# A first self-attention whose layer norm moves into its own tile loop: GpSimd normalises three steps ahead, TensorE transposes beside the projections

## The reference, cut to what matters

```python
x = x + _L0_xattn_ref(_layernorm(x), ctx, ctx, mask, ...)      # phase a
x = x + _L0_attn_ref(_layernorm(x), Wq, bq, Wk, bk)            # phase b, the one changed
x = x + _L0_ffn_ref(_layernorm(x), ...)                        # phase f
...                                                            # phases c, d, g

def _layernorm(x, axis=-1, eps=1e-05):
    m = jnp.mean(x, axis=axis, keepdims=True)
    v = jnp.var(x, axis=axis, keepdims=True)
    return (x - m) / jnp.sqrt(v + eps)

def _L0_attn_ref(x, Wq, bq, Wk, bk):
    q = (x @ Wq + bq)...; k = (x @ Wk + bk)...; v = k
    attn = softmax(einsum('bhnd,bhmd->bhnm', q, k) * C ** (-0.5))
    return einsum('bhnm,bhmd->bhnd', attn, v)...
```

## Time and profile before

| | us |
|---|---|
| time, median of 3 runs (2725.26 to 2728.6) | 2725.66 |
| time of the profiled execution | 2725.43 |
| its span, first to last instruction | 2723.5 |
| mean granted TensorE clock, share of full speed | 0.914 |
| TensorE busy / VectorE / ScalarE / GpSimd | 2278.5 / 1625.7 / 1527.4 / 458.0 |

### The profile page before, as it was taken

The page is one execution under the profiler, slowest core; times in us unless marked ns, Lnnn a source line. Parts: engine busy times, 40 slices in busy tenths (PEclk is TensorE's granted clock), DMA queues, the critical chain, the costliest instruction groups (busy, mean ns, idle before and its releaser), DMA issues. The chain is left out here.

```text
span 2723.5 us, 66405 instructions
## 1 busy us (share of the span) xinstructions
PE 2278.5 (84%) x19431; PEld 1622.9 (60%) x19431; DVE 1625.7 (60%) x5236; ACT 1527.4 (56%) x3786; POOL 458.0 (17%) x1104
## 2 busy tenths in 40 slices
PE   5999999979759997999999999997256217499997
PEld 3777777757536765778778778775115103344443
DVE  5888878867554434665665665665798878701100
ACT  5888888867512224555555555554478737532221
POOL 2545445423213320000000000000000030000000
PEclk9999999989869997999999999998698655699999
DMA  3222222200100002111111111111000000100001
GB/s 90 75 74 71 75 71 72 73 27 1 26 0 0 0 1 90 39 46 43 38 46 43 38 46 43 39 46 34 0 0 1 0 1 4 44 1 0 0 0 31
DMA packets 153177, 90.39 MB, mean 33 GB/s; under 512 B 34033, under 2 KB 151169, under 8 KB 152705
## 3 DMA queue, kind: packets, MB, share of 16 engines
q1 hardware_dynamic: 153088, 89.26, 11.3%
HBM read 68.24 MB, written 20.97 MB: 33 GB/s over the span
## 5 line engine op out<-in xcount | busy, mean ns | idle before, releaser
L667 ACT ACTIVATE a_PR<-a_SM,a_nmx 128x257 f32<-128x257 f32 x512 | 253.4, 499 | 4.0 <-issue 3.3
L1039 ACT ACTIVATE c_PR<-c_SM,c_nmx 128x257 f32<-128x257 f32 x512 | 253.3, 501 | 0.0
L963 PE MATMUL c_bs<-c_cT,c_QP 128*128 128x257 f32 x1024 | 247.9, 386 | 0.8 <-ACT c_QP L1027 0.8
L982 PE MATMUL c_bo<-c_PT,c_C 128*128 128x512 f32 x512 | 240.8, 593 | 2.0 <-DVE c_PT L1099 2.0
L1073 DVE CUSTOM_DVE_ANT_0 c_SM<-c_bs,c_MB 128x257 f32<-128x257 f32 x512 | 215.4, 424 | 17.0 <-PE c_bs L963 14.2
L714 DVE CUSTOM_DVE_ANT_0 a_SM<-a_bs,a_MB 128x257 f32<-128x257 f32 x512 | 188.0, 423 | 44.4 <-PE a_bs L535 39.0
L963 PEld LDWEIGHTS c_bs<-c_cT,c_QP 128*128 128x128 f32 x1024 | 186.0, 192 | 25.8 <-issue 1.7
L947 PEld LDWEIGHTS c_bq<-c_XNT,c_A 128*128 128x128 f32 x1024 | 137.6, 196 | 67.2 <-issue 64.0
L1045 ACT ACTIVATE c_OT<-c_bo 128x512 f32<-128x512 f32 x128 | 76.5, 597 | 173.2 <-PE c_bo L982 173.2
L1099 DVE COPY c_PT<-c_bp 128x512 f32<-128x512 f32 x128 | 88.6, 692 | 121.2 <-PE c_bp L971 121.2
L934 POOL TENSOR_TENSOR c_XL<-quarter,c_PR 128x16 f32<-128x16 f32 x128 | 27.6, 216 | 774.3 <-DVE c_PR L1083 774.3
(11 more groups left out here) (492 smaller groups left out, 5252.4 us busy)
## 6 DMA issues: line engine op xcount, KB each, us to landing
a_C<-in_ctx_dram SPq DMA_DIRECT2D x128, 128.0 KB, 2.1
ctxT_dram<-a_cT SPq DMA_DIRECT2D x128, 128.0 KB, 1.9
c_cT<-ctxT_dram SPq DMA_DIRECT2D x128, 128.0 KB, 2.2
c_C<-in_ctx_dram SPq DMA_DIRECT2D x128, 128.0 KB, 2.1
a_MK<-in_mask_Bx1xSxS_bk_dram SPq DMA_DIRECT2D x128, 32.1 KB, 1.9
X<-in_x_dram SPq DMA_DIRECT2D x4, 512.0 KB, 6.4
g_h<-in_L_ffn_h_w_dram SPq DMA_DIRECT2D x2, 1024.0 KB, 7.9
out_dram<-X SPq DMA_DIRECT2D x1, 2048.0 KB, 8.7
```

The costliest lines, as they stand in the source:

```text
L667: nc.scalar.activation(PR[:, 1 - par, hg, :], SM[:, 1 - par, hg, :], ACT.Exp, bias=nmx[:, 1 - par, hg:hg + 1], accum_out=den[:, 1 - par, h ...
L963: nc.tensor.matmul(b_s[hg][:, 0:SK], QP[:, r // 4 % 2, r % 4, 4 * hg:4 * hg + 4, :], cT[:, r, :], start=True, stop=True).then_inc(s_ps, 1)
L982: last = nc.tensor.matmul(b_o[:, :], C[:, buf, c, :], PT[:, s.r % 2, c, :, :], start=(c == 0), stop=(c == 1))
L1039: nc.scalar.activation(PR[:, 1 - par, hg, :], SM[:, 1 - par, hg, :], ACT.Exp, bias=nmx[:, 1 - par, hg:hg + 1], scale=SCALE, accum_out=den[ ...
```

## The change

`phase_norm` is no longer called in phase b. A new function `normaliser` keeps the chain of small operations (without its last, `shift`), and it now runs at the start of the attention block, on VectorE and ScalarE. GpSimd then normalises one tile a step, three steps ahead of its scores: a subtraction into `XS` and a multiplication of `XS` in place, with a wait on its own semaphore between them. TensorE transposes `XS` into a free quarter of the b_bqk bank, ahead of the projections, and ScalarE copies it into `sh.XNT` after `Q`. Steps begin at -3; the loop now covers steps 4 to 27 instead of 4 to 29.

```diff
-        phase_norm(nc, sh, "b_n_", loads, [b_o, b_t])
-            for g in range(-2, 4):
+            for g in range(-3, 4):
                 step(Step(g, g % 2, NT))
-            with eng.Fori(2, NT // 2 - 1) as j:
+            with eng.Fori(2, NT // 2 - 2) as j:
...
-            for g in range(NT - 2, NT + 1):
+            for g in range(NT - 4, NT + 1):
@@ tensor
+                if s.on(-3):
+                    wait(pe, xs_ok, g + 4)
+                    wait(pe, q_ev, g + 2)
+                    wait(pe, k_ev, g + 2)
+                    wait(pe, xt_ev, g + 3)
+                    nc.tensor.transpose(b_qk[:, 2 * P:3 * P], XS[:, 1 - par, :], sh.ident[:, :]).then_inc(xt_ps, 1)
                 if s.on(-2):
                     wait(pe, q_ev, g + 2)
                     wait(pe, k_ev, g + 2)
+                    wait(pe, xt_ev, g + 3)
@@ scalar
+            stats_on_scalar(act)
+                if s.on(-3):
+                    wait(act, xt_ps, g + 4)
+                    nc.scalar.activation(sh.XNT[:, ds(P * (g + 3), P)], b_qk[:, 2 * P:3 * P], ACT.Copy).then_inc(xt_ev, 1)
@@ gpsimd
+            pool.wait_ge(norm_ok, 1)
             def step(s):
                 g, par = s.g, s.r
+                if s.on(-3):
+                    t = g + 3
+                    wait(pool, xt_ps, g + 2)
+                    nc.gpsimd.tensor_tensor(XS[:, 1 - par, :].unsqueeze(1), sh.X[:, ds(t, 1), :],
+                                            mean[:, ds(t, 1)].unsqueeze(2).broadcast_to([P, 1, D]), ALU.subtract
+                                            ).then_inc(xc_ok, 1)
+                    wait(pool, xc_ok, g + 4)
+                    nc.gpsimd.tensor_tensor(XS[:, 1 - par, :].unsqueeze(1), XS[:, 1 - par, :].unsqueeze(1),
+                                            rstd[:, ds(t, 1)].unsqueeze(2).broadcast_to([P, 1, D]), ALU.mult
+                                            ).then_inc(xs_ok, 1)
                 if s.on(-2):
                     wait(pool, k_ev, g + 3)
@@ vector
+            stats_on_vector(dve)
+            dve.sem_inc(norm_ok, 1)
```

More of the change, by code:

```diff
@@ L289, in tile_stats, with normaliser, on_vector, link @@
     nc.vector.bn_stats(sh.stats[:, ds(t, 1), :], sh.X[:, ds(t, 1), :])
+def normaliser(nc, sh, small, chain, var_ok, std):
+    total, mean, diff, dsq, m2, var, rstd, half = (small[:, i, :] for i in range(8))
+    def on_vector(dve):
+        n = 0
+        def link(ins):
+            nonlocal n
+            n += 1
+            ins.then_inc(chain, 1)
+            dve.wait_ge(chain, n)
+        stats = sh.stats
+        link(nc.vector.tensor_tensor(total, stats[:, :, 1], stats[:, :, 4], ALU.add))
+        link(nc.vector.tensor_scalar(mean, total, 0.5, None, ALU.mult))
+        link(nc.vector.tensor_tensor(diff, stats[:, :, 1], stats[:, :, 4], ALU.subtract))
+        link(nc.vector.scalar_tensor_tensor(out=dsq, in0=diff, scalar=0.25, in1=diff, op0=ALU.mult, op1=ALU.mult))
+        link(nc.vector.tensor_tensor(m2, stats[:, :, 2], stats[:, :, 5], ALU.add))
+        link(nc.vector.scalar_tensor_tensor(out=var, in0=m2, scalar=1.0 / D, in1=dsq, op0=ALU.mult, op1=ALU.add))
+        nc.vector.tensor_scalar(var, var, LN_EPS, None, ALU.add).then_inc(var_ok, 1)
+        dve.wait_ge(std, 1)
+        link(nc.vector.reciprocal(rstd, rstd))
+        link(nc.vector.tensor_tensor(half, rstd, rstd, ALU.mult))
+        link(nc.vector.scalar_tensor_tensor(out=half, in0=half, scalar=-0.5, in1=var, op0=ALU.mult, op1=ALU.mult))
+        link(nc.vector.tensor_scalar(half, half, 1.5, None, ALU.add))
+        link(nc.vector.tensor_tensor(rstd, rstd, half, ALU.mult))
+    def on_scalar(act):
+        act.wait_ge(var_ok, 1)
+        nc.scalar.activation(rstd, var, ACT.Sqrt).then_inc(std, 1)
+    def normed(out, t):
+        return nc.vector.tensor_scalar(out, sh.X[:, ds(t, 1), :], mean[:, ds(t, 1)], rstd[:, ds(t, 1)],
+                                       ALU.subtract, ALU.mult)
+    return on_vector, on_scalar, normed
 def phase_xattn0(nc, sh, ctx_rows, mask, wq, bq, wk, bk, wv, bv, wo, bo):
@@ L1114, in phase_attn0 @@
         sh.XNT = sb("b_XNT", [D, T])
+        small = sb("b_small", [P, 8, NT])
+        XS = sb("b_XS", [P, 2, D])
         Q = sb("b_Q", [D, 2, P])
@@ L1134, in phase_attn0, with run, _ @@
         o_ps, r_ok, n_ok, x_ok = sem("b_o_ps"), sem("b_r_ok"), sem("b_n_ok"), sem("b_x_ok")
-        def loads(sp):
+        chain, var_ok, std, norm_ok = sem("b_chain"), sem("b_var_ok"), sem("b_std"), sem("b_norm_ok")
+        xc_ok, xs_ok, xt_ps, xt_ev = sem("b_xc_ok"), sem("b_xs_ok"), sem("b_xt_ps"), sem("b_xt_ev")
+        stats_on_vector, stats_on_scalar, _ = normaliser(nc, sh, small, chain, var_ok, std)
+        mean, rstd = small[:, 1, :], small[:, 6, :]
+        block = ctx.enter_context(nc.Block())
+        def run(eng, step):
+            for g in range(-3, 4):
+                step(Step(g, g % 2, NT))
+            with eng.Fori(2, NT // 2 - 2) as j:
+                for r in range(2):
+                    step(Step(2 * j + r, r, NT))
+            for g in range(NT - 4, NT + 1):
+                step(Step(g, g % 2, NT))
+        @block.sync
+        def _(sp):
             sp.dma_start(wq_s[:, :], wq).then_inc(w_in, 16)
@@ L1140, in loads @@
                 sp.dma_start(bias[:, i:i + 1], v.rearrange("(d a) -> d a", a=1)).then_inc(w_in, 16)
-        phase_norm(nc, sh, "b_n_", loads, [b_o, b_t])
-        block = ctx.enter_context(nc.Block())
-        def run(eng, step):
-            for g in range(-2, 4):
-                step(Step(g, g % 2, NT))
-            with eng.Fori(2, NT // 2 - 1) as j:
-                for r in range(2):
-                    step(Step(2 * j + r, r, NT))
-            for g in range(NT - 2, NT + 1):
-                step(Step(g, g % 2, NT))
         @block.tensor
```

## The result

The changed kernel took 2735.72 us (median of 10 runs, 2731.72 to 2740.31), the kernel before 2725.62 us on the same chip (10 runs, 2719.53 to 2730.78). The ratio is 1.0039, with an interval of 1.003 to 1.0048: slower by 0.39%. The prediction said 2735 us, slower by 0.35%. The profiled execution took 2737.15 us, 1.85 above its span.

The account below looks back on a forecast made before the run. The middle was taken as a TensorE stage; the change would close a round of 3.65 us a step against 3.08. KS of tile 31 comes 9.7 us later: 2725.4 + 9.7 = 2735 us, range 2727 to 2741.

Parts of the forecast that it names:

- The ring: Attention block: round from projections through KS, KP, GpSimd's pair and transpose to projections sets the step, 3.65 us; chance 0.70.
- projections to KS: Term of the ring: from projections issued on TensorE to KS started on ScalarE, 0.84 us.
- KS to KP: Term of the ring: from KS started on ScalarE to KP started on GpSimd, 0.58 us.
- own semaphore and address instruction: Term of the ring: GpSimd's wait on itself, 0.07, and the address instruction behind it, 0.058; 0.13 us.
- hand-over: Term of the ring: from the end of GpSimd's multiplication to TensorE's transpose, 0.14 us.
- transpose to projections: Term of the ring: TensorE's transpose, 0.11, and an assumed 0.06 before the projections can issue; 0.17 us.
- The middle: KS of tile 4 to KS of tile 31: 26 steps of 3.65 plus 3.1, 98.0 us.
- the start: Block start to KS of tile 4, which comes at 615.3 against 620.30: 5.0 of 10.9 us removed are kept.
- ScalarE's round: Rival: ScalarE's work with the new copy sets the step at 3.3 us; time 2726, no change; chance 0.10.
- All hidden: Rival: all added work falls into idle time, the step stays 3.08 us; time 2720.4; chance 0.10.
- The clock: Rival: TensorE, 81% busy, at low clock for half the middle, 5.6 us more; time 2741; chance 0.07.
- Contention at the addition to X: Rival: GpSimd and VectorE hinder each other at VectorE's addition to X, at most 7.5 us more, 2743; chance 0.03.

Follow-up runs that it names:

- x1: Changed kernel with GpSimd's pair (subtraction, multiplication) four steps ahead instead of three; 2719.89 us, ratio 0.9978 to the kernel before.
- x2: Changed kernel with the subtraction of the mean left out, one GpSimd operation instead of two; 2722.93 us, ratio 0.9988 to the kernel before.
- x8: x1 with ScalarE's copy of the transposed tile moved behind the exponential, TensorE's transpose staying ahead of the projections; 2713.72 us, ratio 0.995 to the kernel before.
- x4: Changed kernel with TensorE's transpose of XS at the end of its step and ScalarE's copy behind the exponential; 2715.48 us, ratio 0.9968 to before.
- x7: x4 with x1's edit, GpSimd's pair four steps ahead; 2717.38 us, ratio 0.9964 to the kernel before.
- x6: x4 with one VectorE tensor_scalar behind DS normalising the tile in place of GpSimd's pair; 2726.8 us, ratio 1.0 to the kernel before.
- x9: x6 with VectorE's normalisation at the end of its step, behind the statistics, four steps ahead; 2718.4 us, ratio 0.9968 to the kernel before.
- x3: Changed kernel with a third GpSimd operation, a multiplication by one with its own wait; 2749.94 us, ratio 1.009 to the kernel before.

## Why the prediction was right

**The ring.** It was forecast at 3.70, taken as 3.65, and measured at 3.89 and 3.65 from KS to KS in the two steps shown, 3.71 in the mean of all 27. By its terms:

| term | predicted | measured, the two steps |
|---|---|---|
| projections to KS | 0.84 | 0.83, 0.83 |
| KS to KP | 0.58 | 0.49, 0.59 |
| KP | 1.04 | 1.00, 1.00 (next begins 0.04 ahead of its end) |
| subtraction, multiplication | 0.40, 0.40 | 0.40, 0.41; 0.40, 0.40 |
| own semaphore and address instruction | 0.13 | 0.18, 0.18 |
| hand-over | 0.14 | 0.33, 0.06 |
| transpose to projections | 0.17 | 0.25, 0.19 |
| sum | 3.70 | 3.89, 3.65 |

The first measured column is the round from KS at 649.21 to KS at 653.10, the second the one from KS at 653.10 to KS at 656.75. The first begins with this row, which the two steps above leave out:

```profile
649.21 0.37 ACT L1274 ACTIVATE b_KS<-b_bqk,b_bias 128x128 f32<-128x128 f32 x1 [0.51 <-PE b_bqk L1237]
```

From key to key the loop's steps take 3.65 and 3.87 in turns, 3.76 in the mean, 0.06 above the sum of 3.70; the written-out steps are shorter (3.33 the first), which makes 3.71 over all 27.

**The middle and the start.** The middle was to be 98.0 and was 100.09: 26 steps of 3.73 instead of 3.65, and a last one of 3.04. The terms that were too small are the waits: own semaphore (+0.05), hand-over (+0.06 in the mean) and transpose to projections (+0.05), less 0.09 for KS to KP, KP and the projections. The start was to keep 5.0 us and kept 5.93: KS of tile 0 came 6.85 after the block's start (7.0 predicted), and the four cold rounds took 15.61 (16.4). These two errors nearly cancel, +2.1 and -0.9. The 1.33 us of phase a, which no step of the forecast covers, brings the profiled execution to 2737.15. That the median, 2735.72, came out 0.7 us from the forecast is therefore partly luck: the errors of the parts cancel, and the ten executions spread over 8.6 us. What is borne out is the round and its length, within 0.06 to 0.08 us a step.

**What it named as signs.** TensorE waits at the transpose of XS in 26 steps, 0.40 each ("0.3 or more in nearly every step"), though the trace names GpSimd in 14 of them only. The pair follows KP without a gap. GpSimd's wait for the keys fell to 42.6/24 = 1.78 from 2.05 (1.7 predicted). KS of tile 4 started at 615.70 (615). ScalarE waits ahead of KS 13.7 us in 26 steps, where the list of before has no such wait. One sign fits only in the mean: KS was to come every 3.6 to 3.7 us, and comes every 3.65 and 3.87 in turns.

**The rivals.** ScalarE's round would have set 3.3, at most 3.36; x1 and x2 stop at 3.29, and x8 shows that ScalarE's copy is in what stops them; but it lay 0.42 under the ring. The prediction's reason for this rival, that ScalarE has almost no idle time in the order of the step, is not so; ScalarE waited 0.83 us a step for TensorE before (waits from 620 to 705 us):

```profile
ACT b_ET L1215 <- PE b_bt L1176: 23.3, 28, 1.1
```

It is into this wait that x4, x7 and x8 put the copy. "All hidden" would have needed 0.36 us for the pair, which took 0.98. The clock did not fall in the middle: TensorE was busy 89.21 of 100.09 us, 89% instead of the 81% reckoned, and the granted clock was 1.00 throughout. The transpose that I had costed at 0.11 us of TensorE's step is recorded with 0.326, as it stands alone behind a wait (groups of the middle, changed kernel):

```profile
L1230 PE MATMUL b_bqk<-ident,b_XS 128*128 128x128 f32 x26 | 8.5, 326 | 4.3 <-issue 2.6 <-POOL b_XS L1311 0.3
```

That is 8.5 of the 12.0 us that TensorE's busy time grew in the middle (77.25 in the earlier trace rows). Contention at the addition to X did not show either: at 651.14 above it takes 0.29 with GpSimd's multiplication from 651.28 beside it, and GpSimd's subtraction kept its length (its multiplication took 0.51 once, at the end of the start, and 0.40 in the median):

```profile
L1307 POOL TENSOR_TENSOR b_XS<-X,b_small x32: 397/401/403, 596.8 to 710.9; 128x128 f32 x24, 128x128 f32<-128x128 f32 x8
```

**What stays open.** Why phase a, with unchanged code, is 1.33 us longer here. x1's start is 2.8 us shorter than the changed kernel's; 2.7 of it lie in the two rounds from KS of tile 0 to KS of tile 2, which take 2.45 and 2.29 us instead of 3.74 each.

## What to carry to other kernels

An engine's idle time pays for new work only if it lies ahead of the point at which the result is needed: write the round down, through every in-order engine that the new work ties together, and compare its sum with the step. Look whether work that runs ahead can run one step further. Here it could without any more buffer, since XS has two halves in both kernels and x1 only fills the other one; that turned +0.39% into -0.22%, and with the copy moved into a wait that stood there anyway -0.50%. The choice of engine mattered less here than the place: on VectorE the work takes a third of the time, and x6 and x9 are still no faster than GpSimd's pair in the right place (x4, x8).

## What the runs showed of the hardware

An fp32 `tensor_scalar` of VectorE from SBUF to SBUF, begun while GpSimd's KP runs, is held until that one ends: 0.81 us instead of 0.34, in every second step of x6's loop. Where the VectorE operation began 0.12 ahead, GpSimd's was 0.08 longer (1.12 for 1.04). The Trainium skill, page GPSIMD Engine Reference, section Key points, names contention with VectorE instructions "in a 2-port perf mode or with two SBUF inputs"; the page VectorE: DVE Perf Modes, section Mode 2×_2P, lists `tensor_scalar` as an operation that can run in such a mode. The first half agrees with x6, though no row shows which mode the operation ran in. For the second, two SBUF inputs, the addition to X beside XS shows no lengthening here: 0.29 us each time. Nor is every VectorE operation that reads SBUF held: the statistics of X (`BATCH_NORM_STATS2`), begun while GpSimd's multiplication runs, take the same 0.29 us as alone, as at 651.58 above.

GpSimd's wait on its own semaphore costs 0.07 us with nothing behind it (x3) and 0.18 where the second operand moves with the tile and an address instruction of 0.052 us follows it; 24 such waits are 4.5 us. The hand-over from GpSimd to TensorE took 0.06 us in one step of a turn and 0.33 in the other, where the trace names issue and not the semaphore; what stands between I did not separate.
